# A two-layer decoder block on one core: second attention without its masked tiles, a sigmoid written with a hyperbolic tangent, and a new table for the order of the steps

## The chip, the cores and the metric

The kernel runs on one core of one Trainium2 chip. The metric is the time of one execution on the device in microseconds, lower is better. PE (TensorE), ACT (ScalarE), DVE (VectorE) and POOL (GpSimd) compute, SP issues most of the transfers.

## The reference

Six blocks follow one another on x of 4 batches x 256 tokens x 256 channels, each added to x and followed by a layer norm: a latent attention with 32 heads, an adjacency from a context, a mixture of eight experts, a second attention with 16 heads, a bilinear block, and a gated feed-forward net. The change touches two of them. The adjacency:

```python
sim = einsum('bhnd,bhmd->bnm', Q, K) / (sqrt(d) * H)      # 4 batches x 256 x 256
threshold = top_k(sim, k)[0][:, :, -1:]                   # k = 76
A = sigmoid(sim) * (sim >= threshold)
A = (A + swapaxes(A, -1, -2)) * 0.5
return (1 - gamma) * adj_raw + gamma * A
```

The second attention, with 16 heads of 16 channels and 256 tokens, causal:

```python
scores = einsum('bthd,bshd->bhts', q, k * scale)
mask = triu(full((s, s), -10000.0), 1)
attn = softmax(scores + mask, axis=-1)
ctx = einsum('bhts,bshd->bthd', attn, v)
```

## The kernel before

The program cuts the work into 526 steps on PE, each with parts on other engines that follow it. `make_plan` declares every step with `stage(step, parts, needs, holds)`: `parts` says which engines work on it and for how many microseconds the planner shall count it, `needs` which steps come first, `holds` which of the 8 PSUM banks and SBUF buffers it takes and who frees them. The order of PE's steps is the table `PE_ORDER` (L196 to 241), written out by hand. `Plan.arrange` walks through it with these durations and lets every other engine take, among the steps that could start about then, the one that PE wants first; `ASIDE` (L243) shifts that preference by step. What comes out is one fixed list per engine, `ORDER`. The planner's durations have no effect on the chip but through these lists. Each engine works through its list, with semaphores where it needs another engine's result.

In `parts`, PE's kind is the shape of the array's tiles: none for 128 rows x 128 columns, `rows64` for two row halves that work at the same time, `cols64` and `cols32` for two or four column groups.

For batch `b` and group `g` of four heads, the second attention takes these steps (`p` is a pair of heads, one in each row half):

- `qkT b g` turns q and k, with extra rows for the mask and the row maxima, into `qT1` and `kT1` (channels on partitions).
- `s1 b g p` (PE, then DVE L2441): scores with queries on partitions. For each of two heads PE multiplies two query tiles of 128 by all 256 keys, then adds the mask to the two diagonal tiles with two small products (`masks_of_heads`). DVE takes the row maximum of the 2 x 256 scores with one `reduce_max`. The tile above the diagonal (first queries, late keys) is computed and masked by an extra row.
- `top_split`, `top_T`: the maxima go through a transpose on PE and small transfers into rows of `qT1`, so that the next product subtracts them.
- `st1 b g p` (ACT L1978): the scores again, keys on partitions, 256 queries for each of two key tiles, with the maxima subtracted and the mask added; ACT takes the exponential of 128 x 512 for each head.
- `pv1 b g`: four heads side by side in column groups of 32; for each head two products in fp32 over the two key tiles, 256 queries wide. An fp32 product shows as two MATMUL records.
- `ctx1_back`, `ctx1_T`, `out1`: transposes, division, and the output projection.

The adjacency, one batch at a time, runs between the steps of the first attention: `adj_sim` (PE, ACT L1875: exp(-sim)), ten rounds `adj_top` on DVE (L2269, L2273), `adj_mask b i` on DVE (L2068 adds 1, L2282 reciprocal, L2075 compares with the threshold and multiplies), `adj_T`.

At the end, `f_mid k` and `f_end k` are the last products of the feed-forward net: the tiles of batch 2 for k = 0, then the two tiles of batch 3. `last_stats` (DVE) needs `f_end 1`, the last `out_stats` needs `f_end 2`.

In the trace every product on PE has L1287 and every transpose L1301 or L1593, since helpers record them. The names after `bank<-` are the moving operand and the weights: `kT,qT` with 64 rows is `s1`, `qT,kT` is `st1`, `mask,halves` is the mask in either, `probs,v_tok` is `pv1`.

## Time and profile before

| | |
|---|---|
| median of 3 runs | 671.9 us (671.45 to 673.34) |
| span of the profiled execution, first to last instruction | 670.2 us |
| time of the profiled execution itself | not listed; the median lies 1.7 us above the span |
| busy: PE, DVE, ACT, POOL | 650.0, 519.6, 499.6, 389.0 us |
| mean granted clock of TensorE | 0.999 of full speed |

Busy time is the union of an engine's records. On PE and DVE a record goes on while the next one has begun, so what an instruction costs in a row of its kind is the distance between two starts, not its duration. The runs are compared by their medians; the span is used to place each sum.

### The profile page before, as it was taken

Reading aid. Unit: us, or ns where it says so; the run is one execution under the profiler, and the core shown is the slowest. Engines: PE = TensorE matmul, PEld = TensorE weight load, DVE = VectorE, ACT = ScalarE, POOL = GpSimd, SP = SyncE. Lnnn points to the kernel's source line nnn. Section 1 sums busy time; section 2 is a strip of 40 time slices with the busy share of each in tenths; the row PEclk is TensorE's granted clock in tenths of the full one; section 3 lists DMA queues with packets and bytes.
Section 4 is the critical chain, followed back from the end, with each engine's and each line's share of the span. In section 5 each row is a group of like instructions: output and inputs, shape, how many; then the busy total and the mean of one; then the engine's idle time right before and its main releaser. Section 6 shows DMA issues by size and latency. Waiting matters only on the chain.

```text
span 670.2 us, 15648 instructions
## 1 busy us (share of the span) xinstructions
PE 650.0 (97%) x5342; PEld 556.9 (83%) x5342; DVE 519.6 (78%) x1684; ACT 499.6 (75%) x1305; POOL 389.0 (58%) x644
## 2 busy tenths in 40 slices
PE   8999999999999999999999999999999999999996
PEld 5779888998898999789977788889788887778886
DVE  3989998997999998567977955556799888849464
ACT  4888786969678785799888766675768686866653
POOL 3488556556655754689769545464772321525842
PEclk9999999999999999999999999999999999999999
DMA  8642022123213120410031020121020000010401
GB/s 331 190 140 63 18 79 73 48 49 95 54 59 113 40 61 21 111 34 2 1 99 60 0 95 1 48 95 40 8 95 4 3 3 4 3 48 1 141 9 56
DMA packets 27299, 40.20 MB, mean 60 GB/s; under 512 B 3914, under 2 KB 19794, under 8 KB 27220
## 3 DMA queue, kind: packets, MB, share of 16 engines
q1 hardware_dynamic: 26932, 38.74, 18.7%
q8 instruction: 43, 0.70, 0.4%
q10 hardware_dynamic: 288, 0.46, 0.3%
q14 instruction: 36, 0.29, 0.1%
HBM read 29.09 MB, written 1.05 MB: 45 GB/s over the span
## 4 chain that ended last, share of the span: by engine, by line
PE 77%; DVE 7%; POOL 4%; ACT 3%; DMA 3%; issue 3%; SPq 2%; DVEq 0%; POOLq 0%; ACTq 0%
PE bank L1287 67%; PE bank L1301 8%; SPq L2800 2%; PE bank L1593 2%; DMA front_pack<-in_front 1%; DMA qT<-xT_plain 1%; POOL probs L2549 1%; POOL qT L2549 1%; DVE u_pair_lo L2072 1%; POOL w_split_lo L2549 1%; POOL probs L2546 1%; ACT x L1736 1%; DVE g_pair_lo L2072 1%; SPq L2721 1%; DVE bn L2095 1%
## 5 line engine op out<-in xcount | busy, mean ns | idle before, releaser
L2546 POOL TENSOR_SCALAR probs<-probs,soft 128x256 f32<-128x256 f32 (+1 forms) x256 | 104.0, 428 | 54.9 <-DVE soft L2231 53.8
L1840 ACT ACTIVATE probs<-probs,soft 128x256 f32<-128x256 f32 (+1 forms) x256 | 113.1, 445 | 20.0 <-DVE soft L2223 19.6
L2549 POOL TENSOR_TENSOR w_split_lo<-w_raw,w_split_hi 128x512 fp32r<-128x512 f32 (+2 forms) x57 | 76.4, 1352 | 52.0 <-ACT w_split_hi L1729 51.7
L1287 PE MATMUL bank<-xT_hi,w_split_hi 128*128 128x512 f32 x256 | 103.5, 404 | 1.6 <-DVE xT_lo L2072 1.1
L1287 PE MATMUL bank<-xT_lo,w_split_hi 128*128 128x512 f32 x256 | 100.5, 393 | 0.0
L1287 PE MATMUL bank<-xT_hi,w_split_lo 128*128 128x512 f32 x192 | 75.4, 393 | 0.0
L2223 DVE CUSTOM_DVE_ANT_0 probs<-bank,front_pack 128x128 f32<-128x128 f32 (+1 forms) x192 | 58.0, 329 | 17.2 <-PE bank L1287 16.4
L1287 PE MATMUL bank<-keyT,qT 128*64 128x64 f32 (+3 forms) x800 | 63.4, 302 | 2.6 <-POOL qT L2549 1.9
L1287 PEld LDWEIGHTS bank<-keyT,qT 128*64 128x64 f32 x800 | 58.0, 137 | 8.9 <-issue 3.3
L1729 ACT ACTIVATE probsT<-bank 128x384 f32<-128x384 f32 x128 | 53.7, 490 | 14.5 <-PE bank L1301 14.1
L1287 PEld LDWEIGHTS bank<-xT_hi,w_split_hi 128*128 128x128 f32 x256 | 48.1, 188 | 14.1 <-issue 2.4
L2549 POOL TENSOR_TENSOR qT<-qT,xT_plain 64x512 f32<-64x512 f32 x34 | 43.8, 1288 | 26.6 <-DMA qT<-xT_plain 25.2
L1287 PEld LDWEIGHTS bank<-xT_lo,w_split_hi 128*128 128x128 f32 x256 | 48.2, 188 | 9.0
L2549 POOL TENSOR_TENSOR probs<-probs 128x512 f32<-128x512 f32 x32 | 42.9, 1356 | 21.3 <-ACT probs L1921 20.6
L1301 PE MATMUL bank<-identity,probs 128*128 128x128 f32 x384 | 50.8, 275 | 1.3 <-POOL probs L2546 1.3
L2549 POOL TENSOR_TENSOR stat<-stat,power 128x2 f32<-128x2 f32 (+1 forms) x25 | 20.5, 821 | 54.0 <-DVE stat L2068 53.4
L1287 PE MATMUL bank<-w_split_hi,g_pair_hi 128*128 128x256 f32 x176 | 50.0, 284 | 1.7 <-DVE g_pair_lo L2072 1.7
L1287 PE MATMUL bank<-w_split_hi,g_pair_lo 128*128 128x256 f32 x176 | 49.6, 282 | 0.0
L1287 PE MATMUL bank<-w_split_lo,g_pair_hi 128*128 128x256 f32 x176 | 49.5, 281 | 0.0
L1840 ACT ACTIVATION_READ_ACCUMULATOR probs<-probs,soft 128x1 f32 x256 | 48.6, 190 | 0.0
L1729 ACT ACTIVATE qT<-bank 64x512 f32<-64x512 f32 (+1 forms) x66 | 39.0, 593 | 12.8 <-PE bank L1287 11.1
L1301 PEld LDWEIGHTS bank<-identity,probs 128*128 128x128 f32 x384 | 42.8, 140 | 5.5 <-POOL probs L2546 3.3
(262 smaller groups left out, 1886.2 us busy)
## 6 DMA issues: line engine op xcount, KB each, us to landing
w_raw<-in_w_front SPq DMA_DIRECT2D x8, 768.0 KB, 4.8
w_raw_heads<-in_w_back SPq DMA_DIRECT2D x8, 640.0 KB, 4.5
qT<-xT_plain SPq DMA_DIRECT2D x68, 64.0 KB, 2.0
qT<-rope_buf SPq DMA_DIRECT2D x32, 64.0 KB, 2.0
w_raw<-in_w_gateT SPq DMA_DIRECT2D x8, 256.0 KB, 2.7
w_raw<-in_w_upT SPq DMA_DIRECT2D x8, 256.0 KB, 3.4
w_raw<-in_w_downT SPq DMA_DIRECT2D x8, 256.0 KB, 3.7
w_raw<-in_L_ffn_Wup SPq DMA_DIRECT2D x7, 256.0 KB, 2.7
```

The source lines that it names most:

```text
L1287: return t.matmul(out, lhsT, rhs, start=start, stop=stop, skip_group_check=shared)
L1301: return t.transpose(out, in_, ident[0:rows, 0:rows])
L1593: ins = t.transpose(out[:, t_ * S + i * P:t_ * S + (i + 1) * P].bitcast(F32R), rows_of_head(rows)[:, i, first:first + P], ident1)
L1729: return s.activation(out, in_, ACT.Copy, **kw)
L1736: ins = s.activation(dst, src, ACT.Identity, bias=stat[place][:, 3, i:i + 1], scale=stat[place][:, 1, i:i + 1])
L1840: ins = s.activation(p[:, at], p[:, at], ACT.Exp, bias=st[:, 0, r:r + 1], scale=-1.0, accum_out=st[:, 1, r:r + 1])
L2072: return v.tensor_tensor(out, in0, in1, op)
L2095: own(v.bn_stats(bn[place][:, i, 0:6], tile))
L2223: v.tensor_tensor_reduce(out=blocks(p[:, at]), in0=blocks(bank_of(("s", b, g, h))[:, at]), in1=mask, scale=-SCALE0, scalar=3.0e38, op0=ALU ...
L2546: return g_.tensor_scalar(out, in0, s1, s2, op0, op1)
L2549: return g_.tensor_tensor(out, in0, in1, op)
L2800: q.dma_start(qT[place][dst:dst + DR // 2, j, :], rope_buf[rope_turns.place[n, g, p]][src:src + DR // 2, 1, :]).then_inc(q_swapped_at[plac ...
```

## The change

1. `s1`: the first query tile meets only the first 128 keys (128 columns in place of 256), and the two mask products fall away. The mask is added on DVE: two `tensor_tensor_reduce` for each head, 128 x 128 and 128 x 256, each adds a triangle `tri1` to the scores, writes the sum back to the same PSUM bank and yields the maximum. `tri1` is a new constant of 128 x 256, loaded as a third part of the load "ln", for which `s1` now waits.
2. `st1`: the second key tile meets only the last 128 queries (128 columns in place of 256), its mask products stay; the exponential covers 384 columns in place of 512.
3. `pv1`: the second key tile's product is 128 columns wide in place of 256.
4. `adj_sim` and `adj_mask`: tanh(sim/2) in place of exp(-sim); DVE compares with the threshold in place, then (tanh + 1) times that; the half goes into the gate's factor. A `tensor_scalar`, a reciprocal and a `scalar_tensor_tensor` become a `tensor_scalar` and a `scalar_tensor_tensor`.
5. `PE_ORDER` and `ASIDE` are new throughout, and four of the planner's durations.

```diff
+LATER1 = (slice(0, S), slice(S, S + P))
+N_LATER1 = S + P
...
-out 0 0, pT 3 0 0, s 2 1 1, pT 3 0 1, pT 2 0 1, s 3 1 1, s 2 1 0, pv 3 0, pv 2 0, s 3 1 0, q 0 1 0, out 2 0,
+out 0 0, pT 2 0 1, out 1 0, pT 3 0 1, s 2 1 1, s 2 1 0, pv 3 0, s 3 1 0, pv 2 0, s 3 1 1, q 0 1 0, out 3 0, pT 2 1 0,
...
-            stage(("adj_mask", b, i), "DVE 2.7", ("adj_top", b, ROUNDS - 1))
+            stage(("adj_mask", b, i), "DVE 0.95", ("adj_top", b, ROUNDS - 1))
...
-                stage(("s1", b, g, p), "PE:rows64 0.49, DVE 1.2", ("qkT", b, g), ("consts",),
+                stage(("s1", b, g, p), "PE:rows64 0.25, DVE 1.15", ("qkT", b, g), ("consts",), ("load", "ln"),
...
-                stage(("st1", b, g, p), "PE:rows64 0.49, ACT:exp 0.97", ("top_T", b, g),
+                stage(("st1", b, g, p), "PE:rows64 0.47, ACT:exp 0.81", ("top_T", b, g),
...
-            stage(("pv1", b, g), "PE:cols32 0.89, ACT 0.3", *[("st1", b, g, p) for p in range(GH // 2)], ("v1", b), *every_expert,
+            stage(("pv1", b, g), "PE:cols32 0.67, ACT 0.3", *[("st1", b, g, p) for p in range(GH // 2)], ("v1", b), *every_expert,
...
+    tri1 = sb("tri1", [P, TB * P])
...
                 for i in range(TB):
                     for j, out in enumerate(outs):
-                        mm(out[:, i * S:(i + 1) * S], qT1[n][head_rows(j), p, i * P:(i + 1) * P],
-                           kT1[n][head_rows(j), p, :], i == 0, False, True)
-                masks_of_heads(mm, outs, 0, scored1)
+                        ins = mm(out[:, i * S:i * S + (i + 1) * P], qT1[n][head_rows(j), p, i * P:(i + 1) * P],
+                                 kT1[n][head_rows(j), p, 0:(i + 1) * P], i == 0, i == TB - 1, True)
+                        if i == TB - 1:
+                            ins.then_inc(scored1.sem, 1)
...
-                        mm(out[:, i * S:(i + 1) * S], kT1[n][head_rows(j), p, i * P:(i + 1) * P],
-                           qT1[n][head_rows(j), p, :], i == 0, False, True)
-                masks_of_heads(mm, outs, 1, st1_ready)
+                        mm(out[:, LATER1[i]], kT1[n][head_rows(j), p, i * P:(i + 1) * P],
+                           qT1[n][head_rows(j), p, i * P:], i == 0, False, True)
+                masks_of_heads(mm, outs, st1_ready)
...
-                        ins = mm(bank_pv[h * HS1:(h + 1) * HS1, 0:S],
+                        ins = mm(bank_pv[h * HS1:(h + 1) * HS1, j * P:S],
                                  v_tok[b % 2][:, j, (g * GH + h) * HV1:(g * GH + h) * HV1 + HS1],
-                                 p[:, j * S:(j + 1) * S], j == 0, j == TB - 1, True)
+                                 p[:, LATER1[j]], j == 0, j == TB - 1, True)
...
-                    s.activation(sim_buf[i][:, 2, :], sim_buf[i][:, 0, :], ACT.Exp, scale=-1.0 / 16).then_inc(sim_exp.sem, 1)
+                    s.activation(sim_buf[i][:, 2, :], sim_buf[i][:, 0, :], ACT.Tanh, scale=1.0 / 32).then_inc(sim_tanh.sem, 1)
...
-                    s.activation(probs[in_probs.place["st1", b, h]][:, :], bank_of(("st1", b, h))[:, :], ACT.Exp,
+                    s.activation(probs[in_probs.place["st1", b, h]][:, 0:N_LATER1], bank_of(("st1", b, h))[:, 0:N_LATER1], ACT.Exp,
...
-                own(ts(sig, sig, 1.0, None, ALU.add))
+                w.wait_ge(*rows_of_sim[b, i])
+                own(ts(sim, sim, best[i][:, at:at + 1], None, ALU.is_ge))
                 w.wait_ge(*own.now)
-                own(v.reciprocal(sig, sig))
-                w.wait_ge(*own.now)
-                stt(adjacency[:, TB * b + i, :], sim, best[i][:, at:at + 1], sig, ALU.is_ge,
-                    ALU.mult).then_inc(adj_masked.sem, 1)
+                stt(adjacency[:, TB * b + i, :], half_turn, 1.0, sim, ALU.add, ALU.mult).then_inc(adj_masked.sem, 1)
...
-                    v.reduce_max(top_tok[top1_turns.place[b, g]][:, top_at(j, p)], two(bank_of(("s1", b, h))), AX).then_inc(top1.sem, 1)
+                    tops = top_tok[top1_turns.place[b, g]][:, top_at(j, p)]
+                    w.wait_ge(*landed("ln"))
+                    for i in range(TB):
+                        scores = bank_of(("s1", b, h))[:, i * S:i * S + (i + 1) * P]
+                        ins = v.tensor_tensor_reduce(out=scores, in0=scores, in1=tri1[:, (TB - 1 - i) * P:], scale=1.0,
+                                                     scalar=-3.0e38, op0=ALU.add, op1=ALU.max, accum_out=tops[:, i:i + 1])
+                    ins.then_inc(top1.sem, 1)
```

How the instructions stand, at the three places that the prediction speaks of. On PE, where the second attention begins, the first `s1` steps, before:

```order
L1287 MATMUL bank<-kT_0,qT_0 128x256 x4
L1287 MATMUL bank<-mask,halves 128x2x64 x4
L1287 MATMUL bank<-kT_0,qT_0 128x256 x4
L1287 MATMUL bank<-mask,halves 128x2x64 x4
L1287 MATMUL bank<-kT_1,qT_1 128x256 x4
L1287 MATMUL bank<-mask,halves 128x2x64 x4
```

and the same place with the change (L1692 are transposes of `qkT 0 3`):

```order
L1386 MATMUL bank<-kT_0,qT_0 128x128 x2
L1386 MATMUL bank<-kT_0,qT_0 128x256 x2
L1386 MATMUL bank<-kT_0,qT_0 128x128 x2
L1386 MATMUL bank<-kT_0,qT_0 128x256 x2
L1692 MATMUL bank<-halves,q_rows 128x128 x4
L1692 MATMUL bank<-halves,k_rows 128x128 x4
```

Each `s1` step has four products in place of eight, two of them half as wide, and the third `s1` step now comes after `qkT 0 3` and `v1 0`.

On DVE, at the same place, what follows the copies of `kT`, before:

```order
L2431 CAST kT_2<-bank 128x512
L2441 TENSOR_REDUCE top_tok<-bank 128x2 x4
L2431 CAST kT_3<-bank 128x512
L2075 SCALAR_TENSOR_TENSOR top_rows<-top_tok,top_rows 128x8
L2441 TENSOR_REDUCE top_tok<-bank 128x2 x2
```

and with the change (the first of them; a pair of heads; `ISA top_tok 128x1` writes out the maximum):

```order
L2529 CAST kT_1<-bank 128x512
L2543 ISA bank,top_tok<-bank,tri 128x128
L2543 ISA top_tok 128x1
L2543 ISA bank,top_tok<-bank,tri 128x256
L2543 ISA top_tok 128x1
L2543 ISA bank,top_tok<-bank,tri 128x128
L2543 ISA top_tok 128x1
L2543 ISA bank,top_tok<-bank,tri 128x256
L2543 ISA top_tok 128x1
```

One instruction for each head has become two main ones and two that write out their result.

On PE, near the end of the program (`q_rows` and `k_rows` are reused buffers of the feed-forward net), before, around `f_end 1`, which is the last three of the six `k_rows` products; the `q_rows` product behind it begins `f_mid 2`:

```order
L1287 MATMUL bank<-w_split_hi,q_rows 128x256
L1287 MATMUL bank<-w_split_hi,k_rows 128x256
L1287 MATMUL bank<-w_split_lo,k_rows 128x256
L1287 MATMUL bank<-w_split_hi,k_rows 128x256 x2
L1287 MATMUL bank<-w_split_lo,k_rows 128x256
L1287 MATMUL bank<-w_split_hi,k_rows 128x256
L1287 MATMUL bank<-w_split_hi,q_rows 128x256
```

and the last nine `k_rows` products with the change, three of `f_mid 1`, three of `f_end 1`, three of `f_end 2`:

```order
L1386 MATMUL bank<-w_split_hi,q_rows 128x256
L1386 MATMUL bank<-w_split_hi,k_rows 128x256
L1386 MATMUL bank<-w_split_lo,k_rows 128x256
L1386 MATMUL bank<-w_split_hi,k_rows 128x256 x2
L1386 MATMUL bank<-w_split_lo,k_rows 128x256
L1386 MATMUL bank<-w_split_hi,k_rows 128x256 x2
L1386 MATMUL bank<-w_split_lo,k_rows 128x256
L1386 MATMUL bank<-w_split_hi,k_rows 128x256
```

`f_end 1` has moved behind `f_mid 2`, so that only the three products of `f_end 2` come after it, where twelve did.

## Rows read from the trace of the kernel before

**Rows 1.** The page: busy time, share of the span and instructions of each engine.
```profile
PE 650.0 (97%) x5342; PEld 556.9 (83%) x5342; DVE 519.6 (78%) x1684; ACT 499.6 (75%) x1305; POOL 389.0 (58%) x644
```

**Rows 2.** The page: the chain of work that ended last, share by engine.
```profile
PE 77%; DVE 7%; POOL 4%; ACT 3%; DMA 3%; issue 3%; SPq 2%; DVEq 0%; POOLq 0%; ACTq 0%
```

**Rows 3.** Timeline of PE: one of its waits, in brackets idle time and releaser.
```profile
283.45 0.87 PE L1287 MATMUL bank<-keyT,qT 128*64 128x192 f32 x8 [1.11 <-POOL qT L2549]
```

**Rows 4.** Busy time of each engine in four stretches, two shown, and their sum.
```profile
core 0: us, PE busy (x) PEld busy (x) DVE busy (x) ACT busy (x) POOL busy (x), PEclk, DMA share, GB/s
...
490.00:515.00 25.00, 24.66 (x282) 21.48 (x282) 24.02 (x52) 18.38 (x42) 11.92 (x17) 1.00 0.21 66
...
565.00:591.00 26.00, 25.19 (x271) 18.32 (x264) 20.12 (x62) 22.98 (x58) 11.95 (x34) 1.00 0.03 9
sum 101.00, PE 99.82 PEld 80.64 DVE 85.06 ACT 79.08 POOL 37.70; mean PE 24.95 PEld 20.16 DVE 21.26 ACT 19.77 POOL 9.42
```

**Rows 5.** Timeline of PE, 518.6 to 521.8: start us, us, what.
```profile
518.68 1.09 PE L1287 MATMUL bank<-probs,v_tok 128*32 128x256 f32 x16
519.71 0.50 PE L1287 MATMUL bank<-kT,qT 64*128 64x256 f32 x4
520.04 0.33 PE L1287 MATMUL bank<-mask,halves 64*128 64x128 f32 x4
520.22 0.45 PE L1287 MATMUL bank<-qT,kT 64*128 64x256 f32 x4
...
520.68 0.45 PE L1287 MATMUL bank<-kT,qT 64*128 64x256 f32 x4
...
521.43 0.34 PE L1287 MATMUL bank<-mask,halves 64*128 64x128 f32 x4
521.70 0.50 PE L1287 MATMUL bank<-bias,ones 128*128 128x512 f32 x1
```

**Rows 6.** Timeline of PE's weight loads in the same stretch.
```profile
519.93 0.30 PEld L1287 LDWEIGHTS bank<-mask,halves 64*128 64x128 f32 x4
520.15 0.30 PEld L1287 LDWEIGHTS bank<-qT,kT 64*128 64x128 f32 x4
520.39 0.31 PEld L1287 LDWEIGHTS bank<-mask,halves 64*128 64x128 f32 x4
```

**Rows 7.** Groups by line and shape: first attention, 256 and 128 columns. Busy, mean ns.
```profile
L1287 PE MATMUL bank<-keyT,qT 128*64 128x256 f32 x200 | 51.4, 385 | 0.0
...
L1287 PE MATMUL bank<-keyT,qT 128*64 128x128 f32 x200 | 38.2, 273 | 0.0
```

**Rows 8.** Timeline of DVE: the maxima of two `s1` steps (four heads).
```profile
504.53 2.47 DVE L2441 TENSOR_REDUCE top_tok<-bank 128x2 f32<-128x512 f32 x4
```

**Rows 9.** Timeline of DVE: one pair of heads in the first attention.
```profile
122.88 0.41 DVE L2223 CUSTOM_DVE_ANT_0 probs<-bank,front_pack 128x256 f32<-128x256 f32 x1
123.21 0.08 DVE L2223 DVE_READ_ACCUMULATOR2_ANT soft<- 128x1 f32 x1
123.21 0.28 DVE L2223 CUSTOM_DVE_ANT_0 probs<-bank,front_pack 128x128 f32<-128x128 f32 x1
...
123.98 0.74 DVE L2269 MAX8 best<-sim 128x8 f32<-128x256 f32 x2
```

**Rows 10.** Tile `sim` of the adjacency: duration ns min/median/max, first and last start.
```profile
L2282 DVE RECIPROCAL sim<-sim x8: 1752/1753/1753, 79.6 to 255.2; 128x256 f32<-128x256 f32 x8
```

**Rows 11.** Timeline of SP: the last issue of load "ln".
```profile
350.68 0.43 SPq L2721 DMA_DIRECT2D ln_rows<-in_L_xattn_ln_beta  x1
```

**Rows 12.** Timeline of DVE and PE at the end.
```profile
662.57 0.29 PE L1287 MATMUL bank<-w_split_hi,k_rows 128*128 128x256 f32 x1
...
663.40 0.42 DVE L2072 TENSOR_TENSOR y<-bank,x 128x256 f32<-128x256 f32 x1
...
664.01 0.28 PE L1287 MATMUL bank<-w_split_hi,k_rows 128*128 128x256 f32 x1
...
664.61 0.41 DVE L2072 TENSOR_TENSOR y<-bank,x 128x256 f32<-128x256 f32 x1
```

208 lines of the change are left out of this document (136 added, 72 removed), and 32 rows, old and new, of the table ASIDE.

## The prediction

> **What bounds the kernel now.** I read the page first. PE is busy for 650.0 of 670.2 us, DVE for 519.6, ACT for 499.6 [rows 1], and the chain that ended last runs through PE for 77% [rows 2]. So PE's list of work sets the time, with 20.2 us in all in which it does nothing: its start, its end, and waits of the kind of [rows 3], 1.1 us for a `qT` tile that POOL still worked on. Next the stretches of the second attention [rows 4]: from 490 to 591 us PE is busy 99.8 of 101.0 us, DVE 85.1. A microsecond less of PE work there is a microsecond less of time as long as nobody else fills up. The one who can is DVE, and it is uneven: 24.0 of 25 us in the first stretch, 20.5 on average in the next two, 20.1 of 26 in the last. ACT (79.1) and POOL (37.7) lose work or keep it.
>
> **What a step costs PE.** In [rows 5] the starts tell more than the durations. From one `kT,qT` at 519.71 over `qT,kT` at 520.22 to the next `kT,qT` at 520.68 a step of either kind takes 0.51 and 0.46 us, the first with a change of tile shape in front. The four mask products take 0.18 of it (520.04 to 520.22). In [rows 6] the weight loads, four in a row, follow four with no gap: the next begin after 0.22 and 0.24 us, before the 0.30 of the records is over, whether their products have 256 columns or 128. A step is eight loads, and they take its 0.46.
>
> **The parts.**
>
> *s1 on PE.* Four products out of eight are left, so four loads. Paced by loads the step costs half of 0.46, so 0.23 goes. Counted by products the mask's 0.18 goes at least, and 0.05 for half the columns of the first pair, the same 0.23. I take 0.23. 32 steps (4 batches, 4 groups, 2 pairs) make **-7.4 us** (ends -5.8 and -7.4).
>
> *pv1 on PE.* 16 records in 1.03 us from 518.68 to 519.71 [rows 5], a change of shape included; four heads side by side, so four records in a row for each head, some 0.23 to 0.26 apiece. Two of the four lose half their 256 columns. In the first attention a record with 256 columns lasts 385 ns and one with 128 lasts 273 [rows 7], 0.11 less. 2 x 0.11 x 16 steps = **-3.5 us** (ends 0, if weight loads paced these too, and -4.2).
>
> *st1 on PE.* It keeps its eight loads, and two of its products lose 128 columns. By the pace of loads it gains nothing; by columns 0.05 for each of 32 steps, -1.6 us. The products come at an uneven pace (0.28 for the scores, 0.18 for the masks), the loads at an even one with no gap to close up, so I take **0**. Here the Trainium skill, "TensorE: Matmul & The Clock Gate", section "Back-to-back issue gap", speaks both ways: its formula for a single product counts columns alone, and beside it stands that in a stream the spacing is set by load and product together. By the formula alone the sum would be 1.7 us lower. The trace is with the second.
>
> *Changes of tile shape.* Counted over the two tables with the kinds in `make_plan`, PE changes shape 149 times before and 134 times after: 79 to 58 up to `xT experts 0`, 9 to 7 in the experts, 61 to 69 from `qkT 0 0` on. One costs 0.09: from the last mask at 521.43 to `bias,ones` at 521.70 are 0.27, where 0.18 was usual [rows 5]. 15 x 0.09 = **-1.4 us** (0 if waits take its place).
>
> *s1 on DVE.* A `reduce_max` costs 0.60: four of them end 2.47 after they begin, each lasting about 0.68 [rows 8], so 1.20 for a pair of heads. In its place come two `tensor_tensor_reduce` for each head. Softmax in the first attention uses the same instruction on the same sizes: a pair of heads with 256 and 128 columns each, accumulators read out, goes from 122.88 to 123.98, 1.10 us [rows 9]. The reads start together with the next instruction and cost nothing. So DVE gains 0.1 for a pair, -3 us in all. One difference: those write to SBUF, these back into the PSUM bank, which no row of before shows on DVE. From above it is bounded by no overlap at all, the records' full length: (0.41 + 0.28 + 2 x 0.08) x 2 = 1.70 for a pair. I take 1.10, since reading from PSUM is the same in both.
>
> *The room that DVE leaves.* PE's work in 490 to 591 falls by 10.9, to 88.9; DVE's goes from 85.1 to 82. That is 92% of the new length on average, and in the first stretch, with 24.0 of 25 busy, DVE cannot follow PE: there 9 pairs give DVE 0.9 back where PE would give 2.6. The new order may level that out, not all of it. I put **+1 us** for it (0 to +4).
>
> *Adjacency.* On DVE eight reciprocals of 1.75 us go [rows 10], 14 us between 79 and 257 us; the added compare stands for the add that was there. All of it lies beside PE, which is busy through that time but for waits. If that cover were gone it would be worth 14; as it is, it is worth what of PE's short waits hangs on a blocked DVE list. **-1 us** (0 to -3). On ACT a tanh replaces an exp one for one; the built lists have ten table loads each in both kernels, so no switch of tables comes with it.
>
> *The third load.* SP issues the other two parts of "ln" at 350.7 [rows 11], and the first `s1` maximum is 140 us later. Zero.
>
> *The end.* `f_end 1` now stands right ahead of `f_end 2`. Before, `f_end 1` ended at 662.86, DVE began the chain for its tile at 663.40 and the one for the last tile at 664.61, 0.3 after the last product's end at 664.29 [rows 12]. With only three products of 0.12 behind it `f_end 1` ends at 663.93, its chain of 1.21 begins then and ends at 665.14: the last tile starts **+0.5 us** later (0 to +0.7).
>
> *ACT's exponentials* fall from 512 to 384 columns, off the path.
>
> **The sum.** -7.4 - 3.5 + 0 - 1.4 + 1 - 1 + 0.5 = -11.8 us, that is a span of 658.4 and, with the 1.7 us by which the median lies over the span, **660.1 us**, 1.8% less. About 0.3%, or 2 us, is what a measurement of this kernel can tell from no change.
>
> **The rivals.**
>
> *DVE takes the whole gain back, and more (slower).* If the reduces overlap with nothing, a pair costs 1.70, 0.50 more than now. 32 x 0.50 puts DVE at 85.1 + 16 = 101.1 busy us in a stretch of 101.0, and DVE cannot be busy all of it: in the last of the four stretches [rows 4] it waits for 5.9 of 26 us while the bilinear block's chains go round. With 5 us of that the second attention is 5 us longer than before and everything waits in `s1`: 671.9 + 5 - 1.4 - 1 + 0.5 = 675. It becomes slower than before from about 1.5 us for a pair. For it speaks that the output goes to PSUM; against it the starts in [rows 9]. The Trainium skill's "VectorE: DVE Perf Modes", section "The DRAIN you can't avoid", says that a VectorE instruction begins only once the pipeline of the one before has emptied, which is this case; the page itself adds that an instruction that isn't held starts earlier. The trace has starts 0.33 after a record of 0.41. Chance 4%.
>
> *Half of the gain stays in waits.* PE is fed just in time today, and the whole order is new. If the write to PSUM costs 0.06 for each of 128 main instructions, 8 us more on DVE, or if `s1` being quick lets PE run into DVE and into the landing of the maxima more often, 4 to 6 us come back as PE waits on `top_tok` and on banks: 665. For it speaks the 24.0 of 25, against it that the later stretches have room. Chance 17%.
>
> *More than the sum.* The columns count in `st1` (-1.6) and DVE's 14 us of relief take three times as much of the waits in the first 300 us (-2 more): 656.5. For it speaks that PE's waits there hang on chains through other engines [rows 3]; against it that this one's releaser is POOL, not DVE. Chance 17%.
>
> *The change doesn't do it.* If the time is set by chains that PE only accompanies, the second attention keeps its length and the kernel stays between 670 and 674. [rows 4] speak against it: PE has no gap there to hide such a chain. Chance 3%.
>
> **How the numbers follow.** The forecast has the remaining 59%, with 658 to 663 as its own range from the ends of its terms. To hold 8 in 10 the range needs most of the upper and the lower rival: 656.5 to 665.5. Faster by over 0.3% are the forecast and the two rivals beside it, 93%; no change 3%; slower 4%.
>
> **What would show it.** In the profile after: `kT,qT` with 128 in place of 256 records, half of them 128 wide, and steps 0.23 apart; `qT,kT` steps still at 0.46; `probs,v_tok` at about 0.8 a step; no masks but 128 records; DVE's new instructions 0.35 and 0.21 apart, in sum 82 busy us over the second attention; that stretch about 91 us long in place of 101; PE busy near 638; the tail behind the last product 6.4 us in place of 5.9. It is wrong if the starts of DVE's pair are over 1.3 us apart, if `st1` falls to 0.41, or if PE's idle time within the second attention is over 4 us where it was 1.2, or if the first 490 us move by more than 3 us either way.

## The result and the profile after

| | median us | lowest to highest | ratio to before (95%) |
|---|---|---|---|
| before | 671.67 | 671.22 to 673.34 | |
| after | 668.49 | 666.44 to 670.20 | 0.994 (0.992 to 0.996) |

The change is a gain, of 3.2 us where 11.8 were forecast. 668.5 lies above the whole range of 656.5 to 665.5. The profiled execution of after took 670.2 us, its span is 668.2. The sum of the prediction was made for the span: 658.4. So 9.8 us have to be found in it. It is the slowest of after's four executions; against the median 8.4 us are missing.

The page of after, busy time and TensorE's granted clock in 40 slices of the span:

```profile
PE 646.3 (97%) x5214; PEld 557.3 (83%) x5214; DVE 512.6 (77%) x1868; ACT 493.6 (74%) x1305; POOL 389.6 (58%) x644
...
PEclk9999999999999999999999799999978999999999
```

PE is busy for 646.3 us. Against [rows 1] that is 3.7 less, where the forecast was 638. The 128 missing products are the masks of `s1`. The chain runs through PE for 80%, 77% before [rows 2]. New is the clock's row: a 7 in one slice, and a 7 and an 8 in two. Before, all 40 digits are 9. Stretches of after tell what is behind them:

```profile
core 0: us, PE busy (x) PEld busy (x) DVE busy (x) ACT busy (x) POOL busy (x), PEclk, DMA share, GB/s
370.00:374.00 4.00, 0.70 (x6) 0.50 (x5) 3.93 (x10) 2.77 (x5) 1.60 (x2) 0.84 0.00 0
374.00:379.60 5.60, 5.55 (x13) 4.43 (x14) 3.96 (x14) 1.04 (x3) 2.64 (x2) 0.50 0.00 0
489.50:491.00 1.50, 0.34 (x5) 0.20 (x3) 1.43 (x8) 1.07 (x3) 1.50 (x3) 1.00 0.00 0
492.20:499.00 6.80, 6.80 (x45) 6.23 (x43) 4.93 (x21) 4.60 (x10) 5.26 (x11) 0.50 0.40 124
507.00:509.20 2.20, 1.24 (x18) 0.93 (x16) 2.20 (x13) 1.95 (x5) 1.60 (x2) 1.00 0.01 3
509.30:512.70 3.40, 3.40 (x29) 2.72 (x29) 3.40 (x18) 1.95 (x6) 0.00 (x0) 0.50 0.00 1
```

They come in pairs: a stretch in which PE stands idle for part of the time, and behind it one in which PE is busy throughout at a granted clock of 0.50, its lower level of 1.2 GHz. The first of them is not in the table: behind an idle time of 1.86 us from 45.82 on, the clock is at 0.50 from 48.5 to 51.9. Together the four are 20.5 us, and the profiled execution of before has nothing like them ahead of its last microseconds. In the clock's row the one at 48.5 still shows as a 9. A busy PE at half its pace looks the same in the busy column, which is why 97% says nothing here.

The milestones of both profiled executions (starts of the first or last product of a kind; the first router product is the first `xT_lo,router_pack`) give the time by stretch; the last column is the prediction's sum, with its changes of tile shape put where it counted them:

| stretch | before | after | difference | forecast |
|---|---|---|---|---|
| up to the first router product | 337.19 | 333.98 | -3.2 | -2.9 |
| experts and first `qkv` | 151.81 | 155.41 | +3.6 | -0.2 |
| second attention (first `q_rows` to last `probs,v_tok`) | 97.37 | 94.25 | -3.1 | -9.2 |
| up to the last `q_rows` | 76.92 | 76.68 | -0.2 | 0 |
| tail | 6.91 | 7.91 | +1.0 | +0.5 |

**The experts.** The timeline of PE in after, with the idle time in brackets:

```profile
374.05 0.77 PE L1386 MATMUL bank<-u_pair_hi,w_split_hi 128*128 128x512 f32 x1 [3.35 <-issue]
374.62 0.63 PE L1386 MATMUL bank<-u_pair_lo,w_split_hi 128*128 128x512 f32 x1
```

This is `e_gate 2 1`. The row names no releaser ("issue"), but the step needs `u_pair_lo`, whose last operation ends at 373.94. The products behind the wait start 0.57 apart and last 0.77 and 0.63, at the lower clock. The timeline of DVE in after says why `u_pair_lo` is late:

```profile
363.26 1.23 DVE L2441 CAST rt_stat<-rt_idx 128x8 f32<-128x8 uint32 x1
364.52 2.48 DVE L2172 TENSOR_TENSOR router_buf<-router_pack,rt_stat 128x32 f32<-128x32 f32 x2
367.04 0.19 DVE L2175 SCALAR_TENSOR_TENSOR router_buf<-router_buf 128x32 f32<-128x32 f32 x1
...
369.45 1.28 DVE L2175 SCALAR_TENSOR_TENSOR router_buf<-router_buf 128x32 f32<-128x32 f32 x1
370.76 0.19 DVE L2456 TENSOR_REDUCE rt_stat<-router_buf 128x4 f32<-128x32 f32 x1
...
371.09 1.65 DVE L2175 SCALAR_TENSOR_TENSOR y<-bank,probs_e,x 128x256 f32<-128x256 f32 x4
372.66 1.28 DVE L2172 TENSOR_TENSOR u_pair_lo<-probs,u_pair_hi 128x512 fp32r<-128x512 f32 x2
```

The router's second half stands ahead of `e_u 2 1` in DVE's list. In before it does so too, and PE waits there for 1.63 us. New are the four operations on `y` (`e_down 1 0`) in between, 1.57 us from 371.09 to 372.66. In before the last two of them end at 366.65, ahead of the router's second half. The router's operations on 8 or 32 columns should be trifles, and one of them takes 0.19 at 367.04. Others take 1.2 to 1.3 each. POOL's timeline at the same time:

```profile
363.16 3.79 POOL L2653 TENSOR_TENSOR w_split_lo<-w_raw,w_split_hi 128x512 fp32r<-128x512 f32 x3
367.36 3.32 POOL L2653 TENSOR_TENSOR probs<-probs 128x512 f32<-128x512 f32 x2 [0.41 <-ACT probs L2021]
```

The operation of 0.19 at 367.04 lies in POOL's gap from 366.95 to 367.36, the next one of 0.19 begins at 370.76, after POOL has ended at 370.68. The slow ones lie beside POOL's `TENSOR_TENSOR` operations. The Trainium skill, "SBUF — State Buffer", section "SBUF: two separate sides", states that a GpSimd operation and a VectorE operation exclude each other for a whole instruction if the VectorE one is in a two-port mode, or has two inputs in SBUF while the GpSimd one reads SBUF. These rows agree for the `TENSOR_TENSOR` ones. The slow `CAST` has one input, and no run here shows whether it is in such a mode.

**The second attention.** The same stretch in three kernels, one row each: before, after, and `swap_sbuf`, an experiment told below, whose clock stays up.

```profile
489.00:586.40 97.40, 95.81 (x1098) 77.88 (x1096) 84.98 (x206) 75.19 (x182) 36.03 (x75) 1.00 0.06 19
```

```profile
489.40:583.70 94.30, 91.31 (x970) 74.27 (x968) 85.62 (x398) 69.36 (x183) 35.77 (x72) 0.95 0.06 20
```

```profile
482.20:572.60 90.40, 87.31 (x970) 70.83 (x968) 82.58 (x398) 69.27 (x183) 35.99 (x73) 1.00 0.07 21
```

PE does the same 970 products in 91.3 us at a mean clock of 0.95 and in 87.3 at 1.00. From start to start, the parts are (idle is the window less PE's busy time):

| us of PE | before | after | `swap_sbuf` |
|---|---|---|---|
| `s1` | 16.2 | 12.0 | 11.1 |
| `st1` | 17.2 | 17.2 | 17.1 |
| `pv1` | 16.8 | 13.7 | 13.3 |
| all else | 46.0 | 48.7 | 45.8 |
| idle between products | 1.6 | 3.0 | 3.1 |

**DVE's pair.** The timeline of DVE in after, one pair of heads in `s1`:

```profile
514.63 0.33 DVE L2543 CUSTOM_DVE_ANT_0 bank<-bank,tri 128x128 f32<-128x128 f32 x1
...
514.88 0.46 DVE L2543 CUSTOM_DVE_ANT_0 bank<-bank,tri 128x256 f32<-128x256 f32 x1
...
515.90 0.14 DVE L2543 DVE_READ_ACCUMULATOR2_ANT top_tok<- 128x1 f32 x1
```

From 514.63 to 515.90 are 1.27 us, the dearest pair; the median of all 32 is 1.23. [rows 9] gave 1.10, and the old maxima in [rows 8] cost 1.20. DVE has 0.6 us more to do in this stretch than before (85.6 against 85.0), where 3 less were forecast.

**The tail.** PE and DVE at the end of after:

```profile
661.40 0.28 PE L1386 MATMUL bank<-w_split_hi,k_rows 128*128 128x256 f32 x1
```

```profile
661.43 0.42 DVE L2172 TENSOR_TENSOR y<-bank,x 128x256 f32<-128x256 f32 x1 [0.55 <-PE bank L1386]
...
662.64 0.41 DVE L2172 TENSOR_TENSOR y<-bank,x 128x256 f32<-128x256 f32 x1
```

The chain of the last tile begins 0.96 after the last product's end at 661.68; in [rows 12] it was 0.32. `f_end 1`'s chain (661.43) is in front, as forecast.

### The profile page after: what moved, and what is told of

Its sections match the earlier page's. It is cut to its first block, busy times and chain, and to the rows that moved or that the text cites. A ratio compares the mean times of both kernels' runs of the same rounds, so it can differ in the third digit from the quotient of the medians.

```text
span 668.2 us, 15602 instructions
## 1 busy us (share of the span) xinstructions
PE 646.3 (97%) x5214; PEld 557.3 (83%) x5214; DVE 512.6 (77%) x1868; ACT 493.6 (74%) x1305; POOL 389.6 (58%) x644
## 4 chain that ended last, share of the span: by engine, by line
PE 80%; DVE 7%; POOL 4%; ACT 3%; issue 3%; SPq 2%; DMA 1%; DVEq 0%; POOLq 0%; ACTq 0%
PE bank L1386 69%; PE bank L1400 8%; PE bank L1692 2%; SPq L2904 1%; DVE bank L2543 1%; POOL probs L2653 1%; DMA qT<-xT_plain 1%; POOL w_split_lo L2653 1%; ACT x L1836 1%; DVE bn L2195 1%; POOL qT L2653 1%; DMA qT<-rope_buf 1%; DVE bilinear L2175 0%; ACT probs L2078 0%; POOL stat L2653 0%
## 5 line engine op out<-in xcount | busy, mean ns | idle before, releaser
L1940 ACT ACTIVATE probs<-probs,soft 128x256 f32<-128x256 f32 (+1 forms) x256 | 113.0, 445 | 11.8 <-DVE soft L2323 11.3
L2653 POOL TENSOR_TENSOR w_split_lo<-w_raw,w_split_hi 128x512 fp32r<-128x512 f32 (+2 forms) x57 | 74.9, 1323 | 47.0 <-ACT w_split_hi L1829 46.9
L1829 ACT ACTIVATE probsT<-bank 128x384 f32<-128x384 f32 x128 | 54.1, 495 | 16.2 <-PE bank L1400 15.8
L2653 POOL TENSOR_TENSOR probs<-probs 128x512 f32<-128x512 f32 x32 | 44.6, 1407 | 32.2 <-ACT probs L2021 31.6
L1386 PE MATMUL bank<-keyT,qT 128*64 128x64 f32 (+3 forms) x768 | 60.1, 301 | 0.7 <-POOL qT L2653 0.7
L1386 PEld LDWEIGHTS bank<-keyT,qT 128*64 128x64 f32 x768 | 55.8, 137 | 4.9 <-issue 1.7
L1940 ACT ACTIVATION_READ_ACCUMULATOR probs<-probs,soft 128x1 f32 x256 | 48.7, 190 | 0.0
L2172 DVE TENSOR_TENSOR u_pair_lo<-probs,u_pair_hi 128x512 fp32r<-128x512 f32 x32 | 27.0, 856 | 27.7 <-ACT probs L2014 27.7
```

The costliest lines, as they stand in the source:

```text
L1386: return t.matmul(out, lhsT, rhs, start=start, stop=stop, skip_group_check=shared)
L1829: return s.activation(out, in_, ACT.Copy, **kw)
L1940: ins = s.activation(p[:, at], p[:, at], ACT.Exp, bias=st[:, 0, r:r + 1], scale=-1.0, accum_out=st[:, 1, r:r + 1])
L2172: return v.tensor_tensor(out, in0, in1, op)
L2653: return g_.tensor_tensor(out, in0, in1, op)
```

## The experiments

Three theories stood at the start. **A:** short idle times let the clock fall, and the slow stretches eat the gain. **B:** the write to PSUM makes DVE's pair dear, and PE waits for DVE. **C:** the new order costs time by itself. All times are medians, all readings of a profile are of one execution of each kernel; each ratio is to runs of before on the same chip (672.2 to 673.0).

### Which part of the change does it

`order_alone`: before with the tables of after.

```diff
-PE_ORDER, ASIDE of before
+PE_ORDER, ASIDE of after
```

> The kernel before with nothing changed but its order: the changed kernel's PE_ORDER and ASIDE tables. If the new order is what costs the gain (theory C), this is slower than before by the 8 us that are missing, near 680. If the clock is what costs it (theory A), the same idle times should appear where this order makes PE wait, and it is slower only as far as the clock shows stretches at 0.5: 672 to 678. If DVE's new instruction is what costs it (theory B), the order is worth nothing of its own: 670 to 673.

700.3 us, ratio 1.042 (1.040 to 1.044). Worse than any theory had it. The longest of its waits, and the stretch behind it:

```profile
227.51 0.90 PE L1396 MATMUL bank<-identity,probs 128*128 128x128 f32 x3 [8.79 <-POOL probs L2641]
```

```profile
221.50:235.10 13.60, 7.59 (x19) 5.30 (x20) 4.14 (x13) 2.59 (x6) 6.53 (x11) 0.50 0.00 0
```

PE idles for 40.9 us in all where it did for 20.2 before, and from within the 8.79 us on the clock stays at 0.50 for 13.6. That the order fits only the cheaper steps is my reading; no run parts it.

`old_order`: after with the tables of before.

```diff
-PE_ORDER, ASIDE of after
+PE_ORDER, ASIDE of before
```

> The changed kernel with the order of the kernel before (both tables). By theory C (the order costs 8 us) this one is near 660 to 662. By theory A the time follows the clock: if the granted clock stays at 1.0 it is near 661, if stretches at 0.5 appear it is 2 to 3.5 us slower for each of 5 to 7 us. By theory B (the maxima of s1 cost 1.26 us for a pair of heads and PE waits for them) it is 667 to 672, with PE waits on top_tok and on free banks in the second attention, since this order was not chosen for the shorter steps.

673.3 us, ratio 1.000 (0.998 to 1.002), slower than all three theories had it; B with its 667 to 672 came nearest. Theory C falls as it was put: without the new order the change is worth nothing, so the order brings about 4 us on balance. The row of its second attention:

```profile
491.90:585.50 93.60, 87.06 (x970) 70.56 (x968) 86.34 (x398) 69.69 (x182) 35.50 (x73) 1.00 0.07 20
```

PE's work is 87.1 us, close to `swap_sbuf`'s 87.3, at full clock, but its idle time from the first `q_rows` to the last `pv1` is 6.5 us where before had 1.6. The waits are for `top_tok` (0.74 at 508.45, 0.52 at 517.32), for `top_rows` and, the longest, for `ctx` (1.76 at 582.88). `narrow_only`, told below, has this order without the edit of `s1`: there PE works for 91.8 us and idles for 1.9. So in the old order the 4.7 us that the new `s1` saves on PE all turn into waits.

`adj_alone`: before with only the adjacency by tanh.

```diff
-activation(Exp, scale=-1/16); ts(+1); reciprocal; stt(is_ge, mult)
+activation(Tanh, scale=1/32); ts(is_ge); stt(+1, mult)
```

> The kernel before with the adjacency's sigmoid by tanh and nothing else, old order. The prediction gave it -1 us (0 to -3): 668.7 to 671.7. If a relieved DVE list is worth more than that it is below 668. If the clock falls here too, slower by 2 us or more. No theory of the three has a large stake; it says which of the first attention's 3 us come from here.

670.3 us, ratio 0.997 (0.995 to 1.000): -1.9 us, within the term's 0 to -3. The stretch up to the first router product is 335.33, 1.9 less than before.

`narrow_only`: before with only `st1`, `pv1` and the exponentials narrowed.

```diff
-mm(out[:, i*S:(i+1)*S], kT1[..], qT1[.., :], ..)
+mm(out[:, LATER1[i]], kT1[..], qT1[.., i*P:], ..)
-mm(bank_pv[.., 0:S], v_tok[..], p[:, j*S:(j+1)*S], ..)
+mm(bank_pv[.., j*P:S], v_tok[..], p[:, LATER1[j]], ..)
```

> The kernel before, in its own order, with only st1 and pv1 narrowed (the exponentials too); s1 keeps its masks on TensorE and its reduce_max on VectorE. By the terms of the prediction pv1 gives 3.5 and st1 nothing: the stretch from the first q_rows to the last probs,v_tok goes from 97.7 to 94.3 us, st1 stays at 0.51 a step, and the time falls by 3 us, 0.5%. The rival: the time won turns into PE waiting for VectorE, which has no work taken from it: PE's idle time in that stretch rises from 1.8 by 1 to 3 us, and the time falls by 1 us or less.

669.3 us, ratio 0.995 (0.993 to 0.997). The stretch goes from 97.4 to 93.9 (from start to start), `pv1` from 16.8 to 13.0, the 32 `st1` steps from 17.2 to 17.0 us. Both terms are right, and PE's idle time rises by 0.3 only.

### The clock and the wait in front of it

`warm`: after with products that compute nothing in front of three waits.

```diff
+if (e, h) == (2, 1): 28 products of 256 columns into e_gate's bank, ahead of its waits
+if (b, g, i) == (0, 0, 1): 12 and 4 products of 128 columns in qkT, ahead of its wait
```

> The changed kernel with products that compute nothing put in front of three waits of PE: 28 of 256 columns ahead of e_gate 2 1 (into its own bank, which it then starts anew), 16 of 128 columns within qkT 0 0. They fill most of the 3.35 us and 1.2 us in which PE stood idle before the granted clock fell to 0.5. By theory A the two stretches at 0.5 that begin at 372.8 and 492.2 (13.7 us, worth about half of it) go away or shrink, and the kernel is 4 to 7 us faster than the changed one: 661 to 665. By theories B and C the clock is a symptom, the waits behind it stay, and the time is 667 to 670.

665.8 us, ratio 0.989 (0.987 to 0.992), 3 us less than after's ratio though it computes more. The stretches at 372.8 and 492.2 are gone; those of 3.4 us at 49.2 and 506.6 stay. This is for A, if just short of its 661 to 665.

`warm_start`: after with 14 idle transposes ahead of `pT 0 0 0`.

```diff
+if (b, g, h) == (0, 0, 0):
+    for _ in range(14): transpose(out[:, 0:P], ident[:, :])
```

> The changed kernel with 14 transposes of the identity, which compute nothing, ahead of the first wait of pT 0 0 0 for POOL, where PE is idle for 1.86 us from 45.82 and the granted clock then shows 0.5 from 48.5 to 51.9. Theory A: that stretch stays at 1.0 and 1 to 2 us are gained, 667. If the clock hangs on something else, the stretch stays and so does the time.

669.8 us (666.8 to 672.4), not told apart from after. The stretch at 48.5 is gone, and the first router product comes 0.5 us earlier, less than expected. One pair of executions does not settle it, but the others agree: in the kernels that share this part with after (not `exp_tail` and `best2`, told below), that product starts at 332.4 to 333.5 without a slow stretch near 48, at 332.9 to 334.0 with one of 3.4 us and at 334.4 to 335.9 with one of 6.8.

`exp_tail`: after with the experts' and the tail's steps in the old order. `best2` is `exp_tail` with the fillers of `warm` in `qkT` and those of `warm_start`.

```diff
-route_lin 0 ... qkv 1 0, f_mid 0 ... f_end 2 of after
+route_lin 0 ... qkv 1 0, f_mid 0 ... f_end 2 of before
```

> The changed kernel with two pieces of the old order put back: the experts' (from route_lin 0 to qkv 1 0, and the shifts of their entries) and the tail's (f_end 1 ahead of f_mid 2). By theory C the experts go from 142.9 us (first router product to the first attn1 product) back to 138.8, as in the kernel before, and the tail behind the last q_rows from 7.9 to 6.9: 5 us faster than the changed kernel, about 663.5. By theory A alone (the clock falls wherever PE idles for over a microsecond) the idle of 3.35 us ahead of e_gate 2 1 goes with its order, so the stretch at 0.5 behind it should go too, and the two cannot be told apart by the time but by the idle time and the clock's rows: 2 us idle, 2.7 clock.

> All that the theories have in one kernel: the changed kernel with the experts' and the tail's old order, the products that compute nothing within qkT 0 0 and ahead of pT 0 0 0. By A and C together no stretch at 0.5 is left but the one at the end and one around 507: 5 us by the order, 1.5 by the clock at the start and 1.5 to 3 at 492, so 659 to 661. If the effects overlap instead of adding up, 663.

676.0 and 674.5 us, ratios 1.005 and 1.003: both expectations missed by over 10 us. The other engines' lists follow from PE's, and here `xT_lo` came late twice:

```profile
338.19 0.41 PE L1375 MATMUL bank<-xT_hi,router_pack 128*8 128x128 f32 x8 [3.12 <-DVE xT_lo L2161]
...
360.96 0.80 PE L1375 MATMUL bank<-xT_hi,w_split_hi 128*128 128x512 f32 x1 [5.29 <-DVE xT_lo L2161]
```

Behind each of the two the clock is at 0.5 for 6.8 us.

`route_swap`: after with two neighbours exchanged, as before had them.

```diff
-e_gate 0 1, route_gate 1, e_down 1 0, e_u 2 1
+e_gate 0 1, e_down 1 0, route_gate 1, e_u 2 1
```

> The changed kernel with two neighbours of its PE order exchanged (e_down 1 0 now ahead of route_gate 1), which in VectorE's list puts e_down 1 0, e_split 0 1 and e_u 2 1 ahead of the router's second half or its parts. If those small operations of the router are what makes u_pair_lo late and PE idle for 3.35 us ahead of e_gate 2 1, the idle falls under 1.5 us there, the stretch at 0.5 behind it goes with it, and 2 to 4 us are gained (665 to 667). The rival: u_pair_lo waits for something else (the u_pair_hi from ScalarE, or a bank), the idle stays between 3 and 4.5, and so does the time.

664.8 us (660.8 to 666.0), ratio 0.990 (0.987 to 0.992). DVE's list now has `u_pair_lo` ahead of the slow operations:

```profile
365.60 2.99 DVE L2172 TENSOR_TENSOR u_pair_lo<-probs,u_pair_hi 128x512 fp32r<-128x512 f32 x2
...
369.18 0.60 DVE L2441 CAST rt_stat<-rt_idx 128x8 f32<-128x8 uint32 x1
```

and PE goes from `g_pair` to `u_pair` with no wait and at full clock:

```profile
369.00 0.39 PE L1386 MATMUL bank<-u_pair_hi,w_split_hi 128*128 128x512 f32 x1
369.24 0.40 PE L1386 MATMUL bank<-u_pair_lo,w_split_hi 128*128 128x512 f32 x1
```

The stretch of the experts takes 149.3 us in place of 155.4. That the place of `u_pair_lo` in DVE's list makes the stall is shown. The profiled execution, 660.8 us, is by far the fastest of the four; a slow stretch of 3.4 us remains in it at 500.8, in the second attention.

### DVE's price and the rest

`out_sbuf2`: after with the masked scores of `s1` written to SBUF, in four buffers.

```diff
-tensor_tensor_reduce(out=scores, in0=scores, in1=tri1[..], ..)
+tensor_tensor_reduce(out=masked1[nth % 4][:, i*P:(2*i+1)*P], in0=scores, in1=tri1[..], ..)
```

> The changed kernel with the masked scores of s1 written to a tile in SBUF (four of them in turn) in place of back into their PSUM bank. Theory B: the write to PSUM is what makes a pair of heads cost DVE 1.26 us in place of the predicted 1.10; here it costs 1.10 and the kernel gains what hangs on it, 1 to 4 us. The rival: PSUM is paid for by the read, and the write's place changes nothing: 1.26 stays and so does the time (within 0.3%).

666.5 us, ratio 0.991 (0.988 to 0.994). Its pair of heads on DVE:

```profile
515.03 0.29 DVE L2547 CUSTOM_DVE_ANT_0 masked<-bank,tri 128x128 f32<-128x128 f32 x1
...
515.24 0.42 DVE L2547 CUSTOM_DVE_ANT_0 masked<-bank,tri 128x256 f32<-128x256 f32 x1
...
516.14 0.08 DVE L2547 DVE_READ_ACCUMULATOR2_ANT top_tok<- 128x1 f32 x1
```

From 515.03 to 516.14 are 1.11 us, the median of all pairs too. The price of the write to PSUM is on average 0.038 for 256 columns, 0.024 for 128 and 0.06 for the read of the accumulator (hidden). Over 64 heads 4.0 us go from DVE. The sum of PE's waits within the stretch stays, 3.1 us against 3.0. What changes is the clock, which never falls there in this execution, and that is hardly chance. `route_swap` and `swap_sbuf` (told below) differ in nothing but this edit. PE's longest wait for `top_tok` in `route_swap`, the clock behind it, and the same wait in `swap_sbuf`:

```profile
499.29 0.50 PE L1386 MATMUL bank<-kT,qT 64*128 64x128 f32 x4 [0.69 <-DVE top_tok L2543]
```

```profile
500.80:504.20 3.40, 3.40 (x33) 2.48 (x33) 2.22 (x9) 1.70 (x5) 0.00 (x0) 0.50 0.01 2
```

```profile
499.34 0.50 PE L1387 MATMUL bank<-kT,qT 64*128 64x128 f32 x4 [0.52 <-DVE top_tok L2547]
```

The wait just before it shrinks too, from 0.27 to 0.16. Of the kernels with the new order of the second attention, the six that write to PSUM (`after`, `warm`, `warm_start`, `exp_tail`, `best2`, `route_swap`) all have a slow stretch of 3.4 us right behind this pair of waits, and the nine that write to SBUF have none there. From the first `q_rows` to the last `probs,v_tok` it is 92.55 us in `route_swap` against 90.12 in `swap_sbuf`, and 92.39 in `warm` against 90.17 in `best3`, which again differ in this edit alone. So B's price is shown, and its effect on PE as well: not as more waiting in sum, but through the clock. How much it is worth varies. By the medians `out_sbuf2` is 0.3% faster than after and `best3` 0.1% faster than `warm`, neither clear of noise, and `swap_sbuf` is 0.9% faster than `route_swap`, which is.

`best3`: `out_sbuf2` with the fillers of `warm`. `swap_warm`: the exchange of `route_swap`, `out_sbuf2`'s edit and the fillers in `qkT` alone.

> The changed kernel with both edits that gained alone: s1's masked scores to SBUF (666.5 alone) and the products that compute nothing ahead of e_gate 2 1 and within qkT 0 0 (665.8 alone). If VectorE's price and the clock are separate causes, they add up but for the part of the second attention that both cured: 662 to 664. If they are one cause (a quicker VectorE only moved the clock's stretches), it stays at 665.5 or above.

> best3 with the exchange of route_swap in place of the 28 products ahead of e_gate 2 1. If the exchange takes the idle away, it needs no filling and this is as fast as best3 or 1 us faster (661 to 664); if it only moves the wait to another place, a stretch at 0.5 shows there and it is slower than best3 by 1 to 3 us.

664.2 (ratio 0.989, 0.985 to 0.992) and 659.5 us (0.981, 0.979 to 0.984), the second below its expected 661 to 664. Taking the stall away is worth 4.7 us more than keeping PE at work through it.

Three variants of `swap_warm` follow. `swap_sbuf` is `swap_warm` without the fillers, `swap_tail` is `swap_warm` with the tail's old order, `wide_s1` is `swap_warm` with the first products of `s1` 256 columns wide, the upper half unread:

```diff
-mm(out[:, i*S:i*S + (i+1)*P], qT1[..], kT1[.., 0:(i+1)*P], ..)
+mm(out[:, i*S:(i+1)*S], qT1[..], kT1[.., :], ..)
```

> swap_warm without the products that compute nothing in qkT 0 0: PE idles there for 1.15 us again. If that wait is enough to bring the clock down, a stretch at 0.5 shows behind it (from about 485) and the second attention is 1 to 3 us longer: 660.5 to 662.5. If the clock fell there only because the experts' stall had come before, it stays at 1.0 and the time is within 0.5 of swap_warm's 659.5.

> swap_warm with the tail's old order (f_end 1 ahead of f_mid 2, and the shifts of the tail's entries taken from before). The prediction priced the new tail at +0.5 us (0 to +0.7); the time behind the last product goes from 6.55 back to 5.90 us: 658.9. By the rival the exchange of the steps ahead of the last product gives that back and it stays at 659.5.

> swap_warm with the first two products of each s1 step 256 columns wide again in place of 128 (what they add is not read; no masks, VectorE as before). If columns pace a step, the first pair's products come 0.165 us apart from the second pair's in place of 0.11: a step costs 0.34 at full clock in place of 0.28, 32 steps cost 1.8 us, about 661.3. If the weight loads pace it, as the prediction had it, nothing changes: steps at 0.28, 659.5.

658.9 (0.980, 0.978 to 0.983), 658.3 (0.978, 0.976 to 0.980) and 658.7 us (0.979), not told apart from one another. The fillers in `qkT` are not needed in this execution: PE idles for 1.17 us there and the clock stays at 1.00. The tail's old order shortens the time behind the last product from 6.56 to 5.91. Against `route_swap` (0.990, 0.987 to 0.992) `swap_sbuf` has the write to SBUF alone: 0.9%, some 6 us. The profiled executions differ by only 2.4 in the second attention, but `route_swap`'s other three have mean clocks of 0.986 to 0.989, its profiled one 0.994. The step of `s1` in `wide_s1`, PE's timeline:

```profile
518.32 0.45 PE L1387 MATMUL bank<-kT,qT 64*128 64x256 f32 x4
518.61 0.34 PE L1387 MATMUL bank<-qT,kT 64*128 64x256 f32 x4
```

From the start of `s1` to that of `st1` are 0.29 us with wide products. In `swap_warm`, with narrow ones, it is 0.28 (PE, then its loads):

```profile
503.67 0.44 PE L1387 MATMUL bank<-kT,qT 64*128 64x128 f32 x4
503.95 0.34 PE L1387 MATMUL bank<-qT,kT 64*128 64x256 f32 x4
...
504.36 0.44 PE L1387 MATMUL bank<-kT,qT 64*128 64x128 f32 x4
```

```profile
503.61 0.30 PEld L1387 LDWEIGHTS bank<-kT,qT 64*128 64x128 f32 x4
503.83 0.31 PEld L1387 LDWEIGHTS bank<-qT,kT 64*128 64x128 f32 x4
```

The columns are free. The four loads of `s1` take 0.22, where [rows 6] had 0.22 and 0.24 for four. By the products' starts the step costs 0.28, but the `st1` step behind it then costs 0.41 in place of 0.46, so that both together take 0.69 (503.67 to 504.36). In before such a pair takes 0.92:

```profile
531.36 0.45 PE L1287 MATMUL bank<-kT,qT 64*128 64x256 f32 x4
...
532.28 0.45 PE L1287 MATMUL bank<-kT,qT 64*128 64x256 f32 x4
```

That is the forecast's 0.23, at the tightest place. Elsewhere it is less. From one `st1` to the next with an `s1` between them it is 0.79 where before had 0.92 to 0.97, and an `s1` step right ahead of another tile shape costs 0.32 to 0.44 us (14 of 32 steps, 0.39 on average, short waits included; 536.30 to 536.68 is one) where before had 0.55 to 0.61 (9 steps, 0.56 on average).

### What the clock costs

Three kernels of the same order: `no_fill` (`swap_tail` without fillers), `stall` (`no_fill` with `u_pair_lo` computed five times more before PE may have it) and `stall_fill` (`stall` with 28 products of 256 columns that compute nothing ahead of the wait).

```diff
+for _ in range(5 if (e, h, i) == (2, 1, DC - 1) else 0):
+    own(tt(up.lo[:, i, :], probs[..], plain(up.hi[:, i, :]), ALU.subtract))
+    w.wait_ge(*own.now)
```

> swap_tail without the products that compute nothing: the changed kernel with e_down 1 0 ahead of route_gate 1, s1's masked scores to SBUF and the tail's old order. By swap_sbuf (658.9) and the tail's 0.65 us: 658.3, no stretch at 0.5 but the one near 48 and the one at the end. If fillers were worth something after all, 659 to 660.

> no_fill with u_pair_lo of e_gate 2 1 computed five times more (the same result) on VectorE before PE may have it: PE idles there for about 3.3 us. By theory A a stretch at 0.5 follows within 3 us of it, and the kernel is slower by the idle time and 1.4 to 2.6 us more: 662.5 to 664.5. If idle time does not bring the clock down, it stays at 1.0 there and the cost is the idle time alone or less: 661 to 661.6.

> stall with 28 products of 256 columns that compute nothing ahead of the same wait (3.4 us at 0.12). By theory A the clock stays at 1.0 behind it and this kernel is 1.4 to 2.6 us faster than stall, though it computes more. If the clock's stretches come from something else, it is as slow as stall or slower.

659.5 (657.9 to 661.3), 665.1 and 664.5 us. `no_fill` lies above its 658.3, though the intervals don't part it from `swap_tail`, and `stall` above its 662.5 to 664.5: the wait came out at 4.1 us where 3.3 were expected. `stall`'s wait, and the clock behind it:

```profile
376.22 0.75 PE L1385 MATMUL bank<-u_pair_hi,w_split_hi 128*128 128x512 f32 x1 [4.13 <-issue]
```

```profile
376.20:379.60 3.40, 3.38 (x8) 2.75 (x9) 3.23 (x19) 0.45 (x1) 0.00 (x0) 0.51 0.00 0
379.60:383.00 3.40, 3.40 (x16) 2.76 (x16) 2.26 (x2) 2.23 (x5) 2.79 (x3) 0.99 0.00 0
```

8 products in 3.4 us, then 16. From the start of `e_gate 2 1` to that of the fourth `e_gate` step behind it, PE needs 36.4 us in `no_fill`, 38.1 in `stall` and 36.5 in `stall_fill`: an idle time of 4.1 us brought 3.4 us at the lower level, which cost 1.7. Against `no_fill` the wait and this make 5.8 us, and the medians differ by 5.6. `out_sbuf2`, with a wait of 4.41 us at this step and 3.4 us at 0.5, needs 38.1 too. With PE at work through the same delay the clock behind it stays at 1.00:

```profile
373.90:410.40 36.50, 36.47 (x204) 31.86 (x205) 27.43 (x58) 27.33 (x43) 17.18 (x13) 1.00 0.15 44
490.00:497.00 7.00, 6.77 (x40) 5.99 (x40) 4.51 (x23) 4.49 (x10) 5.64 (x12) 0.55 0.47 145
```

In the median `stall_fill` is only 0.6 us faster than `stall`, which the intervals don't tell apart and which misses the 1.4 to 2.6. The second row gives a reason: in the profiled execution the clock fell after all, later, behind the 1.15 us wait for `q_rows`, for 6.8 us, and its second attention takes 92.6 us in place of 90.2. Theory A is shown for the long wait, by the profiles; for the short one the fall comes in some executions and not in others.

## Why the prediction was wrong

**The size of `s1` on PE, -7.4.** The step "I take 0.23. 32 steps" failed, by the count and not by the pace. The reading of the loads was right: four take 0.22, and an `s1` and an `st1` step that follow each other take 0.69 in place of 0.92. But that is the best place, and it was put for all 32. A step right ahead of another tile shape saves 0.17, and the new order has 14 such steps where the old had 9. Over all 32 steps measured is -5.1 (16.2 to 11.1 at full clock), 0.16 a step and below the lower end of -5.8. In all 2.3 us are missing. Some 0.5 of them, five more such places at 0.09, are also in the +0.7 that the term for shapes held for this stretch; how the rest divides over the steps isn't worked out.

**`pv1`, -3.5 and `st1`, 0.** Both right: -3.5 (16.8 to 13.3) and -0.1, and -3.8 and -0.2 in `narrow_only`. For `st1` the reading by loads held, the one by columns (-1.6) did not.

**DVE.** "I take 1.10, since reading from PSUM is the same in both" failed: a pair costs 1.23 (1.22 to 1.26) with the output in PSUM and 1.11 in SBUF. The rival "half of the gain stays in waits" had the mechanism (0.06 for each instruction, measured 0.038 and 0.024). In the new order it is not seen in the sum of the waits: PE's idle time in the stretch grew by 1.4 us against the +1 of the sum, and writing to SBUF left it there. In the old order all of `s1`'s gain did turn into waits. And in the new order the longer pair of waits for the maxima is what the slow stretch at 509.3 follows, 2.2 to 2.4 us that are counted under the clock below.

**The clock, no term.** It appears in the prediction nowhere, and is the largest piece. In after's experts the products from 374.05 on need 39.1 us for what takes 36.4 in `no_fill`: 2.7. In its second attention, at the same idle time, 94.25 in place of 90.12 in `swap_sbuf`: 4.1, of which 2.2 to 2.4 hang on the write to PSUM. At the start 0.5 by `warm_start`. Together 7.3 us of the 9.8. This is the account of the profiled execution, with a mean clock of 0.983; the fastest of after's four has 0.990, so it paid less.

**The new order.** Its only priced effects were shapes, "room" and tail. It also moved `e_down 1 0` behind the router's second half, between it and `u_pair_lo`, and a wait of 1.63 us in before became a stall of 3.35 us that I had not looked for: the prediction set the experts at -0.2. Without any wait there the experts' stretch takes 149.3 us, 2.5 less than before; 1.6 of that is before's own wait.

**The parts that held.** Adjacency: -1.9 against -1 (0 to -3). Up to the router -3.2 against -2.9, which is partly luck: in the kernels that share this part with after that milestone lies anywhere from 332.4 to 335.9, and `narrow_only`, which changes nothing ahead of it, has it 0.7 us later than before. The tail: +0.65 behind the last product against +0.5. None of the named ways of being wrong came about. DVE's pair stayed under 1.3, `st1` did not fall over its 32 steps (single ones did, to 0.41), PE's idle time in the second attention stayed under 4, and the first 490 us moved by 0.4, since -3.2 and +3.6 cancel in them. The cause was one that the list did not have.

The sum: 7.3 (clock) + 3.35 (stall) + 2.3 (`s1`) + 0.4 (waits) + 0.5 (tail, milestone to milestone) - 2.3 (experts' order) - 0.8 (up to the router, its clock taken out) = 10.75, of 9.8; the remaining -1 are the shape changes and small differences in the second attention, which I can't part further. Taking the stall out alone does not reach the forecast: `route_swap` takes 664.8 us. With the masked scores written to SBUF as well it does: `swap_sbuf` takes 658.9 us, and `swap_tail` 658.3, 1.6% less than after and 2.2% less than before.

What stays open is why the wait of 1.15 us for `q_rows` is followed by a slow stretch in `after`, `warm_start` and `stall_fill` and not in `order_alone`, `out_sbuf2`, `route_swap`, `swap_sbuf`, `no_fill` and `stall`. That the slow stretches vary between runs of one kernel is seen in after's mean clocks, 0.990 with 666.4 us and 0.983 with 670.2 and 668.7.

## What to carry to other kernels

Where TensorE sets the time, a new order is worth reading for its longest idle time of TensorE, not only for its sum: one late operand cost 3.35 us, and the half-paced stretch behind it 2.7 more, while the busy share stayed at 97%. Look at the clock's row before any other, and find what the late operand's engine does just before; an exchange of two steps was worth more than filling the wait. When half of a step's instructions go, price the half that stays in the middle of a run and at its edge, and count how many steps stand at one. Price an instruction by rows with the same memory on its output side too: a small surcharge on VectorE cost more through TensorE's clock than through waiting.
